# A selective scan of a four-block kernel: its elementwise products taken two units at a time, and one product moved from GpSimd to VectorE

## The chip, the cores and the metric

The kernel runs on one core of a Trainium2 chip. The metric is the device time of one launch in microseconds (us), as a median of runs. The engines are written as in the profile: PE is TensorE (PEld its weight loads), DVE is VectorE, ACT is ScalarE, POOL is GpSimd, and SP is SyncE, whose queue issues the DMAs here.

## What is computed

The kernel runs four blocks one after the other on a 4 x 96 x 64 x 64 image, all in float32. The change lies in the last, a selective scan over four directions of the image (`_L3_conv_ref`):

```python
xs = jnp.stack([x0, x1, x0[..., ::-1], x1[..., ::-1]], axis=1)
x_dbl = jnp.einsum('bkdl,kcd->bkcl', xs, x_proj_weight)
dts, Bs, Cs = jnp.split(x_dbl, [R, R + N], axis=2)
dts = jnp.einsum('bkrl,kdr->bkdl', dts, dt_projs_weight)
A = -jnp.exp(A_logs.astype(jnp.float32)).reshape(K, D, N)
delta = jax.nn.softplus(dts + dt_projs_bias[None, :, :, None])

def step(h, inp):
    u_t, d_t, B_t, C_t = inp
    h = jnp.exp(d_t[..., None] * A) * h + (d_t * u_t)[..., None] * B_t[:, :, None, :]
    y = jnp.einsum('bkdn,bkn->bkd', h, C_t)
    return (h, y)
```

There are 96 channels d, 16 states n, four directions k and, for each of four images, 4096 positions. What follows sums the directions and normalises.

## The kernel before

`selective_scan` cuts the positions into chunks of N = 512. One chunk of one direction is a *step*; there are 4 images x 4 directions x 8 chunks = 128 steps n. In a step the 96 x 16 pairs of channel and state are twelve *units* i of 128 partitions x 512 positions (8 channels x 16 states each). `step` is written out once for each engine and every engine works strictly in the order in which its own `step` lists the work; semaphores tie the engines together. `n1` and `n2` stand for the next step and the one after it, `before` for the previous one.

In words, per step:

- PE: `replicate` (L1669) spreads delta over the 128 partitions of unit i, into one of `DAS` = 3 PSUM tiles `p_da`; since the tile must be free, it waits for scan i - 3. Between the twelve replicates stand: `b_mm` (L1644) and `c_mm` (L1639) of the next step, which replicate B and C; `dt_mm` (L1630), `delta_sum` halves 0 and 1 (L1653 to L1659) and `low_mm` (L1664, L1665), which make delta two steps and one step ahead; four `y_triple` (L1677), each summing the states of three units into `p_y`; and `y_whole` (L1686 to L1690). All of `dt_mm`, `delta_sum`, `low_mm` and `c_mm` write the one PSUM tile `p_bc`, one after the other.
- ACT: `decay` (L1814) takes the exponential in `p_da` for each unit. Between the decays: `delta_and_high` (L1783, L1785), `low` (L1796), `take_y` (L1822 or L1825), the softplus of step n + 2 in pieces (`abs_relu`, `exp_x`, `one_plus`, `kept`, `log_1e`; L1760 to L1776), `c_copy` (L1810) out of `p_bc`, and `b_copy` (L1803).
- DVE: `scan` (L1963) runs the recurrence of a unit, `h` = `p_da` x h + `bu`. Ahead of the scans stand ten `times_b` (L1948), each `bu` = `du_rep` x B for one unit, B being read from PSUM.
- POOL: twelve `times_c` (L1909), each `hc` = `h` x C for one unit; `times_b` (L1902) for units 5 and 11; and `delta_u` (L1891), `du` = delta x u of the next step.
- SP: `restack` (four DMAs that bring delta's two parts into `stacked`, from which PE replicates), `store_du` (one DMA of `du` to DRAM), and twelve `replicate_du` (L1592), which bring `du` back spread over 128 partitions into a ring of `RING` = 8 slots `du_rep`. A slot is written again when its `times_b` has read it.

The delta of step n + 2 goes round the engines in this order: `dt_mm`, `abs_relu` to `log_1e`, `delta_sum` 0 and 1 (half 0 behind `c_copy`), `delta_and_high`, `low_mm`, `low`; only then may the `dt_mm` of the following step write `p_bc`.

## Time and profile before

| | |
|---|---|
| median of 3 runs | 5920.14 us (5917.19 to 5921.82) |
| the profiled execution | 5919.1 us, span of its trace 5917.0 us |
| granted TensorE clock, mean over the span | 0.927 |
| scan, `L1963`, first start to last end | 3253.4 to 5828.9 us |
| busy in the span | PE 4968.7, DVE 4826.2, POOL 3855.9, ACT 2914.8 us |

The scan block is the last 2,600 us but for a short normalisation. A granted clock of 1.00 is 2.4 GHz and 0.50 is 1.2 GHz, the engine's two levels. In a timeline a row is one instruction or several of one kind; matmuls overlap, so from one row of PE the next begins before the first has ended, and the distance of two starts says how long PE was taken.

### The profile page before, as it was taken

The numbers are of one execution on the slowest core, as the hardware profiler recorded it, in microseconds if no ns is written. First come the engines' busy times: TensorE is split into PE (matmuls) and PEld (weight loads), VectorE is DVE, ScalarE is ACT, GpSimd is POOL, SyncE is SP. The second block draws the span as 40 slices with busy tenths as digits, with TensorE's granted clock in tenths as the row PEclk, the third lists the DMA queues.
The fourth block names the chain that finished last, engine by engine and source line by source line (L and its number), as shares of the span: only waits on it lengthen the run. The fifth ranks groups of instructions, "written<-read, shape, count | busy, mean of one in ns | idle before, by whom it ended". The sixth has DMA issues, their size and how long they took to land. (4 is left out here: it accounts for less than half of the span.)

```text
span 5917.0 us, 72829 instructions
## 1 busy us (share of the span) xinstructions
PE 4968.7 (84%) x16018; PEld 2212.0 (37%) x16018; DVE 4826.2 (82%) x4793; ACT 2914.8 (49%) x4462; POOL 3855.9 (65%) x2394
## 2 busy tenths in 40 slices
PE   7999899897699889887068888888888888888887
PEld 1222256463266556555034222222222222222222
DVE  4877633434309999999977999999999999999996
ACT  5777534443201000000023777777777776777776
POOL 0000132322307779777966999999999999999993
PEclk9989899998799889888578999999999999999998
DMA  1000000003864655654041667767676777777773
GB/s 45 0 0 0 7 0 1 0 1 114 229 144 103 135 128 123 136 123 106 0 95 28 182 181 191 187 180 191 187 185 186 187 187 188 186 188 186 186 189 101
DMA packets 340815, 707.92 MB, mean 120 GB/s; under 512 B 46717, under 2 KB 63673, under 8 KB 326745
## 3 DMA queue, kind: packets, MB, share of 16 engines
q1 hardware_dynamic: 340568, 705.15, 47.3%
q8 instruction: 92, 1.51, 0.1%
q14 instruction: 155, 1.26, 0.1%
HBM read 572.97 MB, written 81.67 MB: 111 GB/s over the span
## 5 line engine op out<-in xcount | busy, mean ns | idle before, releaser
L1909 POOL TENSOR_TENSOR l_hc<-l_h,l_c_rep 128x512 f32<-128x512 f32 x1536 | 1927.4, 1273 | 210.5 <-DVE l_h L1963 180.1
L1963 DVE TENSOR_TENSOR_SCAN l_h<-l_p_da,l_h,l_bu 128x512 f32<-128x512 f32 x1120 | 1401.7, 1267 | 6.2 <-ACT l_p_da L1814 4.8
L1814 ACT ACTIVATE l_p_da<-l_p_da,l_a_neg 128x512 f32<-128x512 f32 x1536 | 1008.0, 657 | 724.1 <-PE l_p_da L1669 708.5
L1146 POOL TENSOR_TENSOR l2b_prod<-l2b_v,l2b_attn 128x3136 f32<-128x3136 f32 x114 | 990.1, 8700 | 393.0 <-ACT l2b_attn L1138 369.9
L1669 PE MATMUL l_p_da<-l_stacked,l_pick 96*128 96x512 f32 x1536 | 904.0, 590 | 193.6 <-DVE l_h L1963 184.9
L1948 DVE TENSOR_TENSOR l_bu<-l_du_rep,l_p_b 128x512 f32<-128x512 f32 x1280 | 838.5, 655 | 28.5 <-DMA l_du_rep<-du_scratch 22.6
L1669 PEld LDWEIGHTS l_p_da<-l_stacked,l_pick 96*128 96x128 f32 x1536 | 292.9, 191 | 1165.4 <-DVE l_h L1963 908.1
L1180 DVE TENSOR_REDUCE l2b_osum<-l2b_prod 128x64 f32<-128x3136 f32 x192 | 645.9, 3413 | 2.7
L1677 PE MATMUL l_p_y<-l_hc,l_y_pick 128*32 128x512 f32 x3072 | 560.0, 623 | 72.2 <-POOL l_hc L1909 71.5
L1133 ACT ACTIVATE l2b_logits<-l2b_conv,l2b_this_b 98x512 f32<-98x512 f32 x96 | 66.1, 688 | 912.7 <-PE l2b_conv L1095 912.7
L615 POOL TENSOR_TENSOR l_w_pos_low<-l1a_w_sed,l_w_pos_high 96x1536 fp32r<-96x1536 f32 x1 | 4.1, 4126 | 711.5 <-DVE l_w_fc_high L595 711.5
L1146 DVE TENSOR_TENSOR l2b_prod<-l2b_v,l2b_attn 128x3136 f32<-128x3136 f32 x78 | 386.8, 4959 | 2.5
L1095 PE MATMUL l2b_conv<-l2b_img_high,l2b_w_conv_high 128*98 128x512 f32 x1344 | 349.5, 413 | 33.6 <-DMA l2b_img_low<-qkv_scratch 33.6
L1095 PE MATMUL l2b_conv<-l2b_img_high,l2b_w_conv_low 128*98 128x512 f32 x1344 | 338.8, 403 | 0.0
L1095 PE MATMUL l2b_conv<-l2b_img_low,l2b_w_conv_high 128*98 128x512 f32 x1344 | 337.4, 402 | 0.0
L1902 POOL TENSOR_TENSOR l_pool_bu<-l_du_rep,l_b_sb 128x512 f32<-128x512 f32 x256 | 326.2, 1274 | 0.0
L1963 DVE TENSOR_TENSOR_SCAN l_h<-l_p_da,l_h,l_pool_bu 128x512 f32<-128x512 f32 x224 | 284.5, 1270 | 0.8 <-ACT l_p_da L1814 0.7
L1095 PEld LDWEIGHTS l2b_conv<-l2b_img_high,l2b_w_conv_high 128*98 128x98 f32 x1344 | 226.7, 169 | 140.5 <-issue 31.7
L770 POOL TENSOR_TENSOR l1b_h_h_low<-l1b_h_h,l1b_h_h_high 128x512 fp32r<-128x512 f32 x96 | 125.5, 1319 | 226.8 <-DVE l1b_h_h_high L734 226.8
L1095 PEld LDWEIGHTS l2b_conv<-l2b_img_high,l2b_w_conv_low 128*98 128x98 f32 x1344 | 219.8, 164 | 103.6
L1095 PEld LDWEIGHTS l2b_conv<-l2b_img_low,l2b_w_conv_high 128*98 128x98 f32 x1344 | 219.8, 164 | 102.1
L1297 PE MATMUL l2c_p_x<-l2c_o,l2c_w_proj 96*96 (+1 forms) x64 | 34.6, 626 | 209.7 <-DMA x_back<-x_scratch 209.7
(265 smaller groups left out, 8964.7 us busy)
## 6 DMA issues: line engine op xcount, KB each, us to landing
l_du_rep<-du_scratch SPq DMA_DIRECT2D x1536, 256.0 KB, 3.9
l2b_img_high<-qkv_scratch SPq DMA_DIRECT2D x192, 306.2 KB, 5.5
l2b_img_low<-qkv_scratch SPq DMA_DIRECT2D x192, 306.2 KB, 9.2
l_stacked<-l_parts SPq DMA_DIRECT2D x512, 96.0 KB, 2.7
qkv_scratch<-l2a_strip SPq DMA_DIRECT2D x32, 840.0 KB, 5.1
l2b_v<-qkv_scratch SPq DMA_DIRECT2D x48, 560.0 KB, 16.9
du_scratch<-l_du SPq DMA_DIRECT2D x128, 192.0 KB, 2.2
qkv_scratch<-l2a_v_strip SPq DMA_DIRECT2D x32, 210.0 KB, 4.0
```

What stands on the lines that cost most here:

```text
L770: pool.tensor_tensor(h_hl[1][:, f, :], h[:, f, :], h_hl[0][:, f, :], ALU.subtract).then_inc(s_h_lo, 1)
L1095: mm = pe.matmul(p_conv[n % 2][:], w_conv[w_part][:, g, dx, :], img[x_part][:, hb % 2, row:row + 2 * CP - 1:2, dx:dx + W], start=(at == 0) ...
L1133: act.activation(logits[:, b, CP * ch:CP * (ch + 1), :].rearrange("m p x -> m (p x)"), p_conv[n % 2][:], ACT.Identity, bias=this_b[:]).the ...
L1146: return eng.tensor_tensor(dst.rearrange("q x (dy dx) -> q x dy dx", dx=WIN), window, attn[:, :, r].rearrange("q x (dy dx) -> q x dy dx", ...
L1180: dve.tensor_reduce(osum[:, unit // 2, unit % 2, :], prod[which][:], AX_X, ALU.add).then_inc(s_sum, 1)
L1669: pe.matmul(p_da[i % DAS][:], pick[:, GRP[i] % (Q // DL), :], stacked[:, par, GRP[i] * DL // Q, :], start=True, stop=True).then_inc(s_rep, 1)
L1677: mm = pe.matmul(p_y[par][q * 32:(q + 1) * 32, :], y_pick[:, t, :], hc[:, (G * par + YT * t + q) % HCS, :], start=(t == 0), stop=False)
L1814: act.activation(p_da[i % DAS][:], p_da[i % DAS][:], ACT.Exp, scale=a_neg[:, k * G + GRP[i]:k * G + GRP[i] + 1]).then_inc(s_da, 1)
L1902: pool.tensor_tensor(pool_bu[:, at, :], du_rep[:, ring_at(par, i)], b_sb[:], ALU.mult).then_inc(s_pbu, 1)
L1909: pool.tensor_tensor(hc[:, (G * par + i) % HCS, :], h[:, i, :], c_rep[:, par, :], ALU.mult).then_inc(s_hc, 1)
L1948: dve.tensor_tensor(bu[:, i % BUS, :], du_rep[:, ring_at(par, i)], p_b[par][:], ALU.mult).then_inc(s_bu, 1)
L1963: dve.tensor_tensor_scan(h[:, i, way], p_da[i % DAS][:, way], of, state, ALU.mult, ALU.add).then_inc(s_h, 1)
```

## The change

- `times_b` and `times_c` treat two units (a *duo*, numbered 0 to 5) in one instruction of 128 x 1024 elements; B or C is read twice through an access pattern with a stride of zero (`both`).
- DVE does `times_b` for duos 0, 1, 3 and 4, POOL for duos 2 and 5 (units 4, 5, 10, 11). `pool_bu` is one duo, `bu` two.
- `delta_u` goes from POOL to DVE, behind scan 1. There it reads delta from `p_bc` itself, adds `ln_one` and multiplies by u in one instruction. So `low_mm`, which overwrites `p_bc`, gets a wait for `s_du`, and ACT's `delta_and_high` loses its own.
- DVE's order: `scan` first, then the `times_b` of the duo ahead. POOL's: the last `times_c` of a step stands at the head of the next.
- PE's order: `b_mm` now behind replicate 0, `y_triple` 2 of the step before behind replicate 1, `low_mm` behind replicate 3, `y_triple` 0 behind replicate 7, `y_triple` 1 behind replicate 11 and ahead of `delta_sum` half 1. ACT's `low` stands behind decay 4. Scan and `y_triple` wait for whole duos of `hc`.

```diff
@@ -1424,11 +1424,12 @@
...
-    BUS = 3
...
-    ON_POOL = (5, 11)
-    BU_AHEAD = 4
-    NB = G - len(ON_POOL)
+    DUOS = G // 2
+    ON_POOL = (2, 5)
+    ON_VECTOR = (0, 1, 3, 4)
+    BUS = 2
+    NB, NPB = len(ON_VECTOR), len(ON_POOL)
...
+        def both(a):
+
+            return bass.AP(a.tensor, a.offset, [list(a.ap)[0], [0, 2], [1, N]])
...
-                user, step_of = (i - RING) % G, (i - RING) // G
+                user, step_of = (i - RING) % G // 2, (i - RING) // G
                 if user in ON_POOL:
-                    sp_.wait_ge(s_pbu, len(ON_POOL) * (n + step_of) + ON_POOL.index(user) + 1 + PBU0)
+                    sp_.wait_ge(s_pbu, NPB * (n + step_of) + ON_POOL.index(user) + 1 + PBU0)
                 else:
-                    sp_.wait_ge(s_bu, NB * (n + step_of) + vector_bus(user) + 1 + BU0)
+                    sp_.wait_ge(s_bu, NB * (n + step_of) + ON_VECTOR.index(user) + 1 + BU0)
...
@@ -1661,6 +1666,8 @@
             def low_mm(m):
                 pe.wait_ge(s_hi, m + 1 + HI0)
                 pe.nop(nofuse=True)
+                pe.wait_ge(s_du, m + 1 + DU0)
+                pe.nop(nofuse=True)
                 pe.matmul(p_bc[0:C, :], ident[:], dd[:], start=True, stop=False)
                 pe.matmul(p_bc[0:C, :], minus_r[:], parts[:, 0, :], start=False, stop=True).then_inc(s_lomm, 1)
...
             def y_triple(n, t, par):
-                pe.wait_ge(s_hc, G * n + YT * t + YT + HC0)
+                pe.wait_ge(s_hc, DUOS * n + duos_hold(YT * t + YT) + HC0)
...
                 for i in range(G):
                     replicate(n, i, par)
-                    if before and i == 0:
+                    if n1 and i == 0:
+                        b_mm(n + 1, 1 - par, *n1)
+                    if before and i == 1:
                         y_triple(n - 1, 2, 1 - par)
-                    if n1 and i == 1:
-                        b_mm(n + 1, 1 - par, *n1)
-                    if n1 and i == 2:
+                    if n1 and i == 3:
                         low_mm(n + 1)
                     if before and i == 3:
                         y_triple(n - 1, 3, 1 - par)
@@ -1711,14 +1718,14 @@
                         y_whole(n - 1, *before, 1 - par)
                     if n2 and i == 5:
                         dt_mm(n + 2, *n2, n + 1)
-                    if i == 6:
+                    if i == 7:
                         y_triple(n, 0, par)
                     if n1 and i == 8:
                         c_mm(n + 1, *n1, n2)
-                    if i == 9:
-                        y_triple(n, 1, par)
                     if n2 and i == 10:
                         delta_sum(n + 2, n + 2, 0)
+                    if i == 11:
+                        y_triple(n, 1, par)
                     if n2 and i == 11:
                         delta_sum(n + 2, None, 1)
...
             def delta_and_high(m, par):
                 act.wait_ge(s_d, m + 1)
                 act.nop(nofuse=True)
-                act.wait_ge(s_du, m + DU0)
-                act.nop(nofuse=True)
                 act.activation(dd[:], p_bc[0:C, :], ACT.Identity, bias=ln_one[:])
...
                     decay(n, k, i)
                     if n1 and i == 0:
                         delta_and_high(n + 1, 1 - par)
-                    if n1 and i == 3:
+                    if n1 and i == 4:
                         low(n + 1)
                     if before and i == 5:
                         take_y(n - 1, *before, 1 - par)
...
-            def delta_u(m, b, k, c):
-                pool.wait_ge(s_hi, m + 1 + HI0)
...
-                pool.tensor_tensor(du[:], dd[:], u_of(b, k, c), ALU.mult).then_inc(s_du, 1)
...
+            def times_b(n, duo, par):
+                at, i = ON_POOL.index(duo), 2 * duo
...
+                for j in (i, i + 1):
+                    pool.wait_ge(s_dur[ring_at(par, j)], ring_count(n, par, j))
...
+                user, step_of = 2 * ON_POOL[at - 1], -1 if at == 0 else 0
+                if step_of == 0 or not (isinstance(n, int) and n == 0):
+                    pool.wait_ge(s_h, G * (n + step_of) + user + 2 + H0)
+                pool.tensor_tensor(pool_bu[:], du_rep[:, ring_at(par, i):ring_at(par, i) + 2, :],
+                                   both(b_sb[:]), ALU.mult).then_inc(s_pbu, 1)
...
+            def times_c(n, duo, par):
+                i = 2 * duo
+                if duo == 0:
                     pool.wait_ge(s_ccp, n + 1 + CCP0)
...
+                pool.wait_ge(s_h, G * n + i + 2 + H0)
+                pool.wait_ge(s_ymm, TRIPLES * n + (i + 1 - HCS) // YT + 1 + YMM0)
+                slot = (G * par + i) % HCS
+                pool.tensor_tensor(hc[:, slot:slot + 2, :], h[:, i:i + 2, :], both(c_rep[:, par, :]), ALU.mult).then_inc(s_hc, 1)
...
-                    if i + BU_AHEAD in ON_POOL:
-                        times_b(n, i + BU_AHEAD, par)
-                    if n1 and i == 2:
-                        delta_u(n + 1, *n1)
-                    times_c(n, i, par)
...
+                if before:
+                    times_c(n - 1, DUOS - 1, 1 - par)
+                for duo in range(DUOS - 1):
+                    if duo == 0:
+                        times_b(n, ON_POOL[0], par)
+                    if duo == 2:
+                        times_b(n, ON_POOL[1], par)
+                    times_c(n, duo, par)
...
         @block.vector
...
+            def delta_u(m, b, k, c):
+                dve.wait_ge(s_hi, m + 1 + HI0)
...
+                dve.wait_ge(s_dus, 16 * m + DUS0)
...
+                dve.scalar_tensor_tensor(du[:], p_bc[0:C, :], ln_one[:], u_of(b, k, c), ALU.add, ALU.mult).then_inc(s_du, 1)
...
+            def times_b(n, duo, par):
+                at, i = ON_VECTOR.index(duo), 2 * duo
...
+                for j in (i, i + 1):
+                    dve.wait_ge(s_dur[ring_at(par, j)], ring_count(n, par, j))
+                user, step_of = 2 * ON_VECTOR[(at - BUS) % NB], (at - BUS) // NB
+                if step_of == 0 or not (isinstance(n, int) and n == 0):
+                    dve.wait_ge(s_h, G * (n + step_of) + user + 2 + H0)
+                dve.tensor_tensor(bu[:, at % BUS], du_rep[:, ring_at(par, i):ring_at(par, i) + 2, :],
+                                  both(p_b[par][:]), ALU.mult).then_inc(s_bu, 1)
...
             def step(b, n, k, c, par, n1, n2, before):
...
                 for i in range(G):
-                    if i < G - 1 and i + 1 not in ON_POOL:
-                        times_b(n, i + 1, par)
-                    if i == G - 1 and n1:
+                    scan(n, k, c, i, par)
+                    if n1 and i == 1:
+                        delta_u(n + 1, *n1)
+                    if i % 2 == 0 and i + 2 < G and i // 2 + 1 in ON_VECTOR:
+                        times_b(n, i // 2 + 1, par)
+                    if i == G - 2 and n1:
                         times_b(n + 1, 0, 1 - par)
-                    scan(n, k, c, i, par)
-
+
+            delta_u(0, 0, 0, 0)
             times_b(0, 0, 0)
```

On PE at the end of a step, before: replicate 11, the second half of `delta_sum`, then the next step's replicate 0 (which first waits for `stacked`) and `y_triple` 2.

```order
L1668 REGISTER_ALU
L1669 MATMUL l_p_da<-l_stacked,l_pick 128x512 [waits l3_h]
L1656 MATMUL l_p_bc<-l_kept_e,l_minus 96x512
L1659 MATMUL l_p_bc<-l_one_e,l_ident 96x512 [waits l3_log_of_one_plus_e]
L1668 ISA [waits l3_stacked1]
L1669 MATMUL l_p_da<-l_stacked,l_pick 128x512 [waits l3_h]
L1673 ISA
L1677 MATMUL l_p_y<-l_hc,l_y_pick 32x512 [waits l3_hc]
```

The same place after the change:

```order
L1675 REGISTER_ALU
L1676 MATMUL l_p_da<-l_stacked,l_pick 128x512 [waits l3_h]
L1680 REGISTER_ALU
L1684 MATMUL l_p_y<-l_hc,l_y_pick 32x512 [waits l3_hc]
L1684 MATMUL l_p_y<-l_hc,l_y_pick 32x512 x2
L1661 MATMUL l_p_bc<-l_kept_e,l_minus 96x512
L1664 MATMUL l_p_bc<-l_one_e,l_ident 96x512 [waits l3_log_of_one_plus_e]
L1675 ISA [waits l3_stacked1]
L1676 MATMUL l_p_da<-l_stacked,l_pick 128x512 [waits l3_h]
```

`y_triple` 1 (the L1684 rows), which stood two units earlier, now lies between replicate 11 and `delta_sum` half 1; the next step's replicate 0 stands behind both.

On PE around `low_mm` (the matmuls on `l_dd` and `l_parts`), before:

```order
L1669 MATMUL l_p_da<-l_stacked,l_pick 128x512 [waits l3_h]
L1662 REGISTER_ALU
L1664 MATMUL l_p_bc<-l_dd,l_ident 96x512 [waits l3_delta_and_high]
L1665 MATMUL l_p_bc<-l_parts,l_minus_r 96x512
L1668 REGISTER_ALU
L1669 MATMUL l_p_da<-l_stacked,l_pick 128x512 [waits l3_h]
L1673 REGISTER_ALU
L1677 MATMUL l_p_y<-l_hc,l_y_pick 32x512 [waits l3_hc]
L1677 MATMUL l_p_y<-l_hc,l_y_pick 32x512 x2
L1668 REGISTER_ALU
```

and after:

```order
L1675 REGISTER_ALU
L1676 MATMUL l_p_da<-l_stacked,l_pick 128x512 [waits l3_h]
L1667 REGISTER_ALU
L1671 MATMUL l_p_bc<-l_dd,l_ident 96x512 [waits l3_delta_and_high,l3_du]
L1672 MATMUL l_p_bc<-l_parts,l_minus_r 96x512
L1680 REGISTER_ALU
L1684 MATMUL l_p_y<-l_hc,l_y_pick 32x512 [waits l3_hc]
L1684 MATMUL l_p_y<-l_hc,l_y_pick 32x512 x2
L1675 REGISTER_ALU
L1676 MATMUL l_p_da<-l_stacked,l_pick 128x512 [waits l3_h]
```

`low_mm` has moved behind replicate 3, so that it is followed at once by `y_triple` 3 and then by replicate 4, and it waits for `l3_du` too.

On DVE at the head of a step, where that `du` comes from (scans are printed as SCALAR_TENSOR_TENSOR on `l_h`); after the change, from `delta_u` on:

```order
L1949 ISA [waits l3_du_stored]
L1949 SCALAR_TENSOR_TENSOR l_du<-l_p_bc,l_ln_one,x_back 96x512
L1967 REGISTER_ALU
L1968 REGISTER_ALU [waits l3_da]
L1975 REGISTER_ALU [waits l3_hc]
L1978 SCALAR_TENSOR_TENSOR l_h<-l_p_da,l_h,l_bu 128x512 [waits l3_bu]
L1967 REGISTER_ALU
L1978 SCALAR_TENSOR_TENSOR l_h<-l_p_da,l_h,l_bu 128x512 [waits l3_bu,l3_hc,l3_da]
L1967 REGISTER_ALU
L1968 REGISTER_ALU [waits l3_da]
L1971 ISA [waits l3_hc]
L1978 SCALAR_TENSOR_TENSOR l_h<-l_p_da,l_h,l_pool_bu 128x512 [waits l3_pool_bu]
```

Before, every scan but two had a `times_b` of one unit ahead of it and `delta_u` stood on POOL:

```order
L1947 REGISTER_ALU [waits l3_du_replicated2]
L1948 TENSOR_TENSOR l_bu<-l_du_rep,l_p_b 128x512 [waits l3_h]
L1955 REGISTER_ALU [waits l3_da]
L1960 REGISTER_ALU [waits l3_hc]
L1963 SCALAR_TENSOR_TENSOR l_h<-l_p_da,l_h,l_bu 128x512 [waits l3_bu]
L1947 REGISTER_ALU [waits l3_du_replicated3]
L1948 TENSOR_TENSOR l_bu<-l_du_rep,l_p_b 128x512 [waits l3_h]
L1955 REGISTER_ALU [waits l3_da]
```

## Rows read from the trace of the kernel before

**Rows 1.** Windows, one step: busy time of PE, PEld, DVE, ACT, POOL, then granted clock, DMA.

```profile
4522.64:4542.72 20.08, 17.56 (x57) 5.73 (x55) 20.08 (x23) 14.56 (x25) 18.68 (x16) 1.00 0.69 192
```

**Rows 2.** Timeline of DVE: start us, us, engine, line, operation, tiles.

```profile
4522.64 1.26 DVE L1963 TENSOR_TENSOR_SCAN l_h<-l_p_da,l_h,l_bu 128x512 f32<-128x512 f32 x1
4523.84 0.65 DVE L1948 TENSOR_TENSOR l_bu<-l_du_rep,l_p_b 128x512 f32<-128x512 f32 x1
...
4527.96 2.44 DVE L1963 TENSOR_TENSOR_SCAN l_h<-l_p_da,l_h,l_bu 128x512 f32<-128x512 f32 x2
```

**Rows 3.** Timeline of PE, first half of the step.

```profile
4520.61 1.06 PE L1677 MATMUL l_p_y<-l_hc,l_y_pick 128*32 128x512 f32 x6
4521.60 0.50 PE L1669 MATMUL l_p_da<-l_stacked,l_pick 96*128 96x512 f32 x1
...
4522.40 0.80 PE L1669 MATMUL l_p_da<-l_stacked,l_pick 96*128 96x512 f32 x1
4523.03 1.02 PE L1664 MATMUL l_p_bc<-l_dd,l_ident 96*96 96x512 f32 x2
...
4524.13 0.39 PE L1669 MATMUL l_p_da<-l_stacked,l_pick 96*128 96x512 f32 x1
...
4525.73 0.50 PE L1669 MATMUL l_p_da<-l_stacked,l_pick 96*128 96x512 f32 x1 [0.23 <-DVE l_h L1963]
4526.07 1.87 PE L1690 MATMUL l_p_y<-l_y_sum,l_ident 96*96 96x512 f32 x2
```

**Rows 4.** Timeline of ACT in the same step.

```profile
4525.14 0.58 ACT L1796 ACTIVATE l_parts<-l_p_bc 96x512 fp32r<-96x512 f32 x1
...
4528.21 0.66 ACT L1814 ACTIVATE l_p_da<-l_p_da,l_a_neg 128x512 f32<-128x512 f32 x1 [1.28 <-PE l_p_da L1669]
...
4529.81 0.66 ACT L1814 ACTIVATE l_p_da<-l_p_da,l_a_neg 128x512 f32<-128x512 f32 x1
...
4531.86 0.66 ACT L1814 ACTIVATE l_p_da<-l_p_da,l_a_neg 128x512 f32<-128x512 f32 x1 [0.21 <-PE l_p_da L1669]
...
4535.81 0.58 ACT L1810 ACTIVATE l_c_rep<-l_p_bc 128x512 f32<-128x512 f32 x1
...
4540.79 0.66 ACT L1814 ACTIVATE l_p_da<-l_p_da,l_a_neg 128x512 f32<-128x512 f32 x1 [1.29 <-PE l_p_da L1669]
```

**Rows 5.** Timeline of PE, end of the step.

```profile
4536.64 1.07 PE L1653 MATMUL l_p_bc<-l_relu_x,l_ident 96*96 96x512 f32 x2 [0.37 <-ACT l_c_rep L1810]
```

**Rows 6.** Groups of POOL by shape (count, busy us, mean ns of one).

```profile
L1909 POOL TENSOR_TENSOR l_hc<-l_h,l_c_rep 128x512 f32<-128x512 f32 x1536 | 1927.4, 1273 | 210.5 <-DVE l_h L1963 180.1 <-issue 24.4
L1146 POOL TENSOR_TENSOR l2b_prod<-l2b_v,l2b_attn 128x3136 f32<-128x3136 f32 x114 | 990.1, 8700 | 393.0 <-ACT l2b_attn L1138 369.9 <-DVE l2b_osum L1180 23.2
...
L955 POOL TENSOR_TENSOR l2a_strip<-l2a_qk,l2a_strip 96x1024 fp32r<-96x1024 f32 x32 | 73.8, 2307 | 109.5 <-DVE l2a_strip L915 109.5
```

**Rows 7.** Groups of DVE by shape.

```profile
L747 DVE SCALAR_TENSOR_TENSOR x_front<-l1b_h_p_x,l_cols,l1b_h_x 96x512 f32<-96x512 f32 x32 | 36.1, 1129 | 54.1 <-PE l1b_h_p_x L645 54.1
...
L1343 DVE SCALAR_TENSOR_TENSOR l2c_x<-l2c_p_x,l2c_cols,x_back 96x512 f32<-96x512 f32 x32 | 23.5, 734 | 15.7 <-PE l2c_p_x L1297 15.7
```

**Rows 8.** A window in which the granted clock fell (columns as in rows 1).

```profile
4563.00:4566.00 3.00, 3.00 (x9) 0.98 (x9) 1.95 (x3) 0.68 (x2) 0.00 (x0) 0.50 0.09 23
```

**Rows 9.** Timeline of PE about this window.

```profile
4562.51 0.51 PE L1669 MATMUL l_p_da<-l_stacked,l_pick 96*128 96x512 f32 x1 [1.97 <-DVE l_h L1963]
4562.94 1.93 PE L1677 MATMUL l_p_y<-l_hc,l_y_pick 128*32 128x512 f32 x6
...
4566.29 0.80 PE L1669 MATMUL l_p_da<-l_stacked,l_pick 96*128 96x512 f32 x1
```

**Rows 10.** Timeline of the DMA queue SP (rows merged).

```profile
4527.14 2.45 SPq L1566 DMA_DIRECT2D l_stacked<-l_parts  x4
...
4532.22 12.88 SPq L1592 DMA_DIRECT2D l_du_rep<-du_scratch  x11
```

**Rows 11.** The page: DMA issues, KB each, median us to landing.

```profile
l_du_rep<-du_scratch SPq DMA_DIRECT2D x1536, 256.0 KB, 3.9
```

66 lines of the change are left out of this document (25 added, 41 removed).

## The prediction

> **What bounds the kernel now.** The sum is made against the profiled execution, 5919.1 us, of which the trace spans 5917.0; it lies 1 us under the median, so both are read as one. I read a window of one step first [rows 1]: 20.08 us, the distance of two scans of unit 0. DVE is busy for all of it, POOL for 18.68, PE for 17.56, ACT for 14.56, and the granted clock is 1.00. The 128 steps make 2,570 of the 5,917 us; all else in the kernel is untouched.
>
> DVE's timeline [rows 2] shows how its step adds up. The next instruction starts 1.20 us after a scan's start, and two scans in a row show 2.44 with one full 1.26 in it, so 1.18; I take 1.19. Twelve are 14.28, and the rest of 20.08 over ten `times_b` is 0.58 each. DVE sets the pace.
>
> But PE and ACT have a chain of their own through the one tile `p_bc`, and it is nearly as long. Its two slack places: replicate 4 waits 0.23 for DVE [rows 3], and the decay 7 waits 0.21 on PE [rows 4]. I look at this chain because the change touches it twice.
>
> **What the change takes from DVE.** Ten `times_b` of 0.58 are 5.8. The trace has no 128 x 1024 product on DVE. A 512 product costs 0.58 here, of which I can't tell the fixed part. Two of them, 1.16, are the upper bound; twice as many elements can't cost less than 1.5 times (0.87), which I call an estimate. I take 1.11, near the upper end, since 0.58 for 512 elements leaves little that is fixed. Four are 4.44. `delta_u` on DVE is new: the same operation with the same operands in PSUM and SBUF took 734 ns in one block and 1129 in another [rows 7]. I take 0.74 for its result and 0.62 until DVE's next instruction, as a recorded 0.65 product has 0.58. DVE's sum: 14.28 + 4.44 + 0.62 = 19.34, 0.74 less than 20.08. If DVE still set the pace, 128 x 0.74 = 95 us would be saved.
>
> A rule of the Trainium skill promises more: "VectorE: DVE Perf Modes", section "The TRN2 errata", says that a large tile pays the fixed latency once where many small ones pay it each time, and its formula has 151 cycles of it, 0.157 us. By that, an estimate from the page, eight units in four instructions instead of eight save 0.63 us in a step, where my 4.44 against 8 x 0.58 = 4.64 saves 0.20; DVE's step would be 18.9. The trace speaks against so much: at 0.58 for the whole of a 512 product its fixed part must lie mostly beside the scan.
>
> **POOL.** Fifteen instructions go, eight of 1024 elements come. The nearest row is 2307 ns for 96 x 1024 [rows 6]; two of 1273 would be 2.55. Eight are 18.5 to 20.4 us. `times_b` of duo 5 now waits for scan 5, since `pool_bu` is one duo, and behind it stand `times_c` 2 to 4; POOL is idle there in any case if a step takes more than 20.4.
>
> **The chain through `p_bc`.** Here two things are added.
>
> First, `low_mm` now waits for `delta_u`, which DVE reaches only behind scan 0, `times_b` 1 and scan 1; scan 0 needs decay 0, which needs replicate 0, which stands on PE behind `delta_sum` half 1. Behind `low_mm` on PE are queued `y_triple` 3 and replicate 4, for which decay 4 and scan 4 wait; then `y_whole` and `dt_mm`, for which the whole softplus on ACT waits.
>
> Second, `y_triple` 1 now stands between replicate 11 and `delta_sum` half 1, that is inside the chain; before it stood where PE had time.
>
> The ring, from scan 0 to the next scan 0, in a step whose `y_whole` reads the turned `y_sum`:
>
> - scan 0, `times_b` 1, scan 1: 1.19 + 1.11 + 1.19 = 3.49
> - `delta_u` 0.74, and 0.15 until PE has passed its wait: 0.89 (an estimate: PE starts 4536.64 - 4535.81 - 0.58 = 0.25 behind ACT's `c_copy` [rows 4, 5], with two waits to pass there)
> - `low_mm` until the matmul behind it: 4523.03 to 4524.13, 1.10 [rows 3]
> - `y_triple` 3 until the replicate behind it: 4520.61 to 4521.60, 0.99 [rows 3]
> - replicate 4, `y_whole`, replicate 5 until decay 5: 4525.73 to 4528.21, 2.48 [rows 3, 4]
> - ACT from decay 5 to `c_copy`: 4528.21 to 4535.81, less the wait of 0.21: 7.39 [rows 4]; ACT has no other gap there
> - from `c_copy` over `delta_sum` 0, replicate 11, `delta_sum` 1 and replicate 0 to decay 0: 4535.81 to 4540.79, 4.98 [rows 4, 5]
> - `y_triple` 1, new in there: 0.99
> - decay 0 until the scan: 0.66 and some 0.04
>
> Sum: 3.49 + 0.89 + 1.10 + 0.99 + 2.48 + 7.39 + 4.98 + 0.99 + 0.70 = **23.0 us**, 3.7 above what DVE needs. In the other half of the steps (directions 0 and 2, contiguous `y_sum`) the way over decay 4, `low` (0.58 until the next, rows 4), `dt_mm` and replicate 6 to decay 6 decides: replicate 4 to decay 4 0.53, `low` 0.58, wake 0.75, `dt_mm` 1.10, replicate 0.53, then 4529.81 to 4535.81 less 0.21, 5.79: 9.28 in the place of 2.48 + 7.39, **22.4 us**. The mean is 22.7. (0.53 is replicate to its decay, 0.75 `low`'s duration with its wake: both estimates from 0.50 in rows 3 and 0.58 in rows 4.)
>
> As a check, the same sum for the kernel before: without `y_triple` 1, and with decay 0 to `low_mm` being 2.3 (decay 0 stands 20.08 ahead of 4540.79, `low_mm` at 4523.03) instead of 0.70 + 3.49 + 0.89 = 5.08, plus replicate 3 ahead of `y_triple` 3 (0.3) gives 23.0 - 0.99 - 2.8 + 0.3 = 19.5, and 0.44 of waits on DVE and PE makes the 20.08 seen.
>
> **What TensorE's clock does to it.** In the ring PE stands idle twice for long. Replicate 3 may start when scan 0 has ended, 1.3 us behind its start, and is done at 1.8; `low_mm` comes at 3.49 + 0.89 = 4.4, 2.6 us later. `delta_sum` half 0 comes at 17.1 (the ring's sum up to there and 0.8), replicate 10 is done at about 15.1, behind scan 7: 2.0 us. Now PE's waits in a step are 0.23 and 0.37 [rows 3, 5] and the clock is 1.00 [rows 1]. At a place where PE paused 1.97 us for a scan [rows 9], the granted clock in the 3 us behind it was 0.50, which is 1.2 GHz [rows 8]. There `y_triple`, a replicate and `b_mm` took 4562.94 to 4566.29, 3.35 us; at 2.4 GHz they take 4520.61 to 4522.40, 1.79 [rows 3]. One fall thus costs 1.56 us where PE is on the ring, and behind both pauses it is. Two falls in a step: 22.7 + 3.1 = **25.8 us**. 128 x (25.8 - 20.08) = 733, and 5919 + 733 = **6652 us**.
>
> [...]
>
> **DMA.** `low` comes later, 8 us behind scan 0 instead of 3. From `restack` to the first `replicate_du` are 4532.22 - 4527.14 = 5.1 us [rows 10], under 1 more to the second, 3.9 to land [rows 11]: about 18 us behind scan 0, when `times_b` 0 is due at 18.7 (4.3 ahead of the next scan 0: `times_b` 0, scan 11 and some 2.0 of waits for decays 11 and 0) in the 23.0 us ring and later with the clock. It is just hidden; if it landed 1 to 2 us late, the step would be up to 1 us longer.
>
> **Rivals.**
>
> 1. *The ring at full clock.* Pauses of 2 to 2.6 us need not lower the clock each time. 22.7 us a step: 5919 + 128 x 2.63 = **6256 us**.
> 2. *DVE keeps the pace, faster than before.* This needs PE to find `low_mm`'s wait met early, or a ring 3.4 us shorter than summed. It decides as soon as the ring is under 19.34. Then 5919 - 95 = **5824 us**. For it speaks that DVE is busy for 100% of a step now; against it, that each term of the ring is in fixed order.
> 3. *Only half of it binds*, `y_triple` 1 in the chain but not the wait: 19.5 + 0.99 = 20.5, **about 5970 us**; with both errors of the sum, no change.
> 4. *POOL slows down.* In the attention block the 128 x 3136 product took 8700 ns [rows 6], 2.77 ns for an element, while DVE worked beside it. At that rate a duo costs 2.84 and a step 22.7, no more than the ring: 6256 us or the forecast. The Trainium skill ("GPSIMD Engine Reference", "Specifications") puts such contention down to DVE instructions with two SBUF inputs; by that rule it stays away, since every DVE instruction of this scan reads one operand from PSUM.
> 5. *The clock stays at half.* PE's parts of the ring (1.10 + 0.99 + about 2 + about 4 + 0.99) are 9 us and would double: some 31 us, **7300 us**.
>
> **How the numbers follow.** Ring with falls of the clock (24.0 to 28.5 us a step, one to three falls and the bounds of the duo and of `delta_u`): 0.62. Rival 1: 0.24. Rival 5: 0.06. Rival 2: 0.04. Rival 3 or no change: 0.04. Rival 4 adds nothing of its own below that. The predicted time is the likeliest's, 6652. The range from 6220 (22.4 us a step throughout) to 7000 (28.5) leaves out about 0.15. About 0.2% is what a measurement of this kernel can tell from no change. Faster 0.05, same 0.02, slower 0.93.
>
> **What would show it.** In the profile after: a distance of scans of unit 0 over 22 us; PE waiting some 2.6 us on DVE's `delta_u` in front of `low_mm`; ACT's decay 4 waiting about 4 us on PE; DVE idle in front of scan 4 (about 1.2 us) and scan 0 (about 1.8 us), released by ACT's `p_da`; the granted clock in the scan near 0.88 (two falls of 3 us to half in 25.8) instead of 1.00; POOL idle several us a step. If DVE is busy for nearly the whole step the ring was wrong; if the clock stays near 1.00, rival 1 was right. A duo's product on DVE near 1.2 us recorded and on POOL near 2.3 would confirm the prices.

## The result: 15.5% slower

| | before | after |
|---|---|---|
| median, us | 5920.69 (4 runs, 5917.19 to 5921.82) | 6836.83 (4 runs, 6827.68 to 6844.59) |
| profiled execution, its span | 5919.1, 5917.0 | 6830.65, 6828.8 |
| mean granted clock of the span | 0.927 | 0.838 |
| distance of two scans of unit 0, mean of 127 | 20.13 | 27.32 |

The ratio is 1.1548, with a 95% interval of 1.1528 to 1.1568. The scan alone accounts for it: 128 x (27.32 - 20.13) = 920 us, and the medians differ by 916. The forecast was 6652 in a range from 6220 to 7000, so the direction and the range were right, and the size was 185 us short.

### The profile after

The page, costliest groups (line, engine, operation, out<-in, shapes, count | busy us, mean ns | idle before, releaser). They answer to [rows 6, 7].

```profile
L1911 POOL TENSOR_TENSOR l_hc<-l_h,l_c_rep 128x1024 f32<-128x1024 f32 x768 | 1794.1, 2349 | 583.3 <-DVE l_h L1978 544.0
L1819 ACT ACTIVATE l_p_da<-l_p_da,l_a_neg 128x512 f32<-128x512 f32 x1536 | 999.6, 657 | 1670.6 <-PE l_p_da L1676 1655.7
...
L1978 DVE TENSOR_TENSOR_SCAN l_h<-l_p_da,l_h,l_pool_bu 128x512 f32<-128x512 f32 x448 | 572.8, 1279 | 529.4 <-ACT l_p_da L1819 523.4
...
L1901 POOL TENSOR_TENSOR l_pool_bu<-l_du_rep,l_b_sb 128x1024 f32<-128x1024 f32 x256 | 606.5, 2369 | 561.3 <-DVE l_h L1978 521.4
...
L1960 DVE TENSOR_TENSOR l_bu<-l_du_rep,l_p_b 128x1024 f32<-128x1024 f32 x512 | 612.6, 1196 | 13.7 <-DMA l_du_rep<-du_scratch 13.0
L1671 PE MATMUL l_p_bc<-l_dd,l_ident 96*96 96x512 f32 x256 | 214.2, 933 | 320.5 <-DVE l_du L1949 320.5
```

Read it from the idle times. `low_mm` (L1671) waits 320.5 us on `l_du`; that is 2.5 us in each of the 128 steps, and a wait that the kernel before does not have. ACT's decays wait 1656 us on the replicates, POOL's two groups more than 1,000 on the scans, and the scans of DVE 790 on ACT (523 of them in the group shown, 227 and 39 in two more groups of scans). Everyone waits for the next engine of the ring, and no engine is the bound. Only 13 us of DVE's idle time ahead of its pairs comes from a DMA: the transfers of `du_rep` stayed hidden, as the forecast had them.

A stretch of 1,000 us of the scan; the columns are start:end, length, then busy time (and count) of PE, PEld, DVE, ACT, POOL, the granted clock, the DMA share and GB/s. The kernel before:

```profile
4500.00:5500.00 1000.00, 872.99 (x2735) 287.56 (x2733) 994.37 (x1095) 726.09 (x1210) 926.22 (x747) 0.99 0.71 186
```

The kernel after:

```profile
4500.00:5500.00 1000.00, 791.75 (x1985) 247.42 (x1985) 706.89 (x615) 513.82 (x874) 674.79 (x290) 0.78 0.52 136
```

DVE falls from 99% busy to 71%, and the clock from 0.99 to 0.78. So the change takes its work off the engine that bound the kernel, and that engine then stands idle for more than it saved.

Within one step, the timeline of PE (start us, duration, ..., and in brackets the idle time ahead with its releaser):

```profile
4509.88 0.77 PE L1676 MATMUL l_p_da<-l_stacked,l_pick 96*128 96x512 f32 x2
4513.19 2.00 PE L1671 MATMUL l_p_bc<-l_dd,l_ident 96*96 96x512 f32 x2 [2.54 <-DVE l_du L1949]
...
4515.54 1.93 PE L1684 MATMUL l_p_y<-l_hc,l_y_pick 128*32 128x512 f32 x6
...
4524.13 0.80 PE L1676 MATMUL l_p_da<-l_stacked,l_pick 96*128 96x512 f32 x1
4526.23 0.80 PE L1676 MATMUL l_p_da<-l_stacked,l_pick 96*128 96x512 f32 x1 [1.30 <-DVE l_h L1978]
4528.12 1.99 PE L1658 MATMUL l_p_bc<-l_relu_x,l_ident 96*96 96x512 f32 x2 [1.09 <-ACT l_c_rep L1815]
```

And the same step in slices (columns as above):

```profile
4508.80:4513.00 4.20, 1.85 (x9) 0.52 (x8) 4.19 (x5) 2.72 (x5) 2.68 (x2) 0.90 0.14 16
4513.00:4516.00 3.00, 2.81 (x6) 0.88 (x9) 2.40 (x3) 0.00 (x0) 2.34 (x2) 0.50 0.51 153
4516.00:4520.00 4.00, 4.00 (x11) 1.19 (x6) 0.89 (x1) 1.17 (x2) 1.92 (x1) 0.63 0.00 0
4520.00:4524.00 4.00, 3.33 (x13) 1.14 (x12) 4.00 (x5) 3.84 (x7) 1.23 (x1) 1.00 0.52 148
4524.00:4528.00 4.00, 1.72 (x4) 0.48 (x2) 4.00 (x4) 3.97 (x8) 4.00 (x3) 0.73 0.47 154
4528.00:4532.00 4.00, 3.88 (x5) 1.30 (x5) 2.92 (x3) 0.93 (x2) 4.00 (x2) 0.50 1.02 251
4532.00:4536.00 4.00, 4.00 (x10) 1.02 (x10) 1.28 (x1) 0.66 (x1) 1.65 (x2) 0.50 1.01 243
```

Two falls, one behind each group of pauses: 2.54 us ahead of `low_mm`, then 1.30 and 1.09 us ahead of replicate 10 and `delta_sum` half 0. The clock is at its lower level of 1.2 GHz (0.50) as soon as the work resumes. `y_triple`, six products, takes 1.93 us there and 1.06 at 2.4 GHz. A slice's mean clock gives its time at half: (1 - 0.90) x 2 x 4.2 = 0.84, then 3.0, then (1 - 0.63) x 2 x 4 = 2.96, so the first fall holds for 6.8 us, and the second for 2.16 + 8 = 10.2 and more. What it does downstream, on ACT and then on DVE:

```profile
4518.23 0.66 ACT L1819 ACTIVATE l_p_da<-l_p_da,l_a_neg 128x512 f32<-128x512 f32 x1 [6.57 <-PE l_p_da L1676]
```

```profile
4519.11 1.28 DVE L1978 TENSOR_TENSOR_SCAN l_h<-l_p_da,l_h,l_pool_bu 128x512 f32<-128x512 f32 x1 [3.70 <-ACT l_p_da L1819]
```

### The profile page after: what moved, and what is told of

Same layout as the page of the kernel before. It is cut to its first block and busy times, and to the rows that moved or that the text cites. A ratio compares the mean times of both kernels' runs of the same rounds, so it can differ in the third digit from the quotient of the medians.

```text
span 6828.8 us, 69015 instructions
## 1 busy us (share of the span) xinstructions
PE 5476.9 (80%) x16018; PEld 2329.0 (34%) x16018; DVE 4769.8 (70%) x4153; ACT 2881.8 (42%) x4462; POOL 3861.0 (57%) x1498
## 3 DMA queue, kind: packets, MB, share of 16 engines
q14 instruction: 136, 1.11, 0.1%
## 5 line engine op out<-in xcount | busy, mean ns | idle before, releaser
L1911 POOL TENSOR_TENSOR l_hc<-l_h,l_c_rep 128x1024 f32<-128x1024 f32 x768 | 1794.1, 2349 | 583.3 <-DVE l_h L1978 544.0
L1978 DVE TENSOR_TENSOR_SCAN l_h<-l_p_da,l_h,l_bu 128x512 f32<-128x512 f32 x896 | 1107.8, 1267 | 322.4 <-ACT l_p_da L1819 227.2
L1676 PE MATMUL l_p_da<-l_stacked,l_pick 96*128 96x512 f32 x1536 | 1071.6, 725 | 230.0 <-DVE l_h L1978 227.8
L1978 DVE TENSOR_TENSOR_SCAN l_h<-l_p_da,l_h,l_pool_bu 128x512 f32<-128x512 f32 x448 | 572.8, 1279 | 529.4 <-ACT l_p_da L1819 523.4
L1901 POOL TENSOR_TENSOR l_pool_bu<-l_du_rep,l_b_sb 128x1024 f32<-128x1024 f32 x256 | 606.5, 2369 | 561.3 <-DVE l_h L1978 521.4
L1684 PE MATMUL l_p_y<-l_hc,l_y_pick 128*32 128x512 f32 x3072 | 708.1, 776 | 4.4 <-POOL l_hc L1911 4.4
L1676 PEld LDWEIGHTS l_p_da<-l_stacked,l_pick 96*128 96x128 f32 x1536 | 330.8, 216 | 1034.4 <-DVE l_h L1978 552.4
L1960 DVE TENSOR_TENSOR l_bu<-l_du_rep,l_p_b 128x1024 f32<-128x1024 f32 x512 | 612.6, 1196 | 13.7 <-DMA l_du_rep<-du_scratch 13.0
L1671 PE MATMUL l_p_bc<-l_dd,l_ident 96*96 96x512 f32 x256 | 214.2, 933 | 320.5 <-DVE l_du L1949 320.5
L1658 PE MATMUL l_p_bc<-l_relu_x,l_ident 96*96 96x512 f32 x256 | 248.5, 1073 | 148.2 <-ACT l_c_rep L1815 141.5
```

The source lines that it names most:

```text
L1658: pe.matmul(p_bc[0:C, :], ident[:], relu_x[:], start=True, stop=False)
L1671: pe.matmul(p_bc[0:C, :], ident[:], dd[:], start=True, stop=False)
L1676: pe.matmul(p_da[i % DAS][:], pick[:, GRP[i] % (Q // DL), :], stacked[:, par, GRP[i] * DL // Q, :], start=True, stop=True).then_inc(s_rep, 1)
L1684: mm = pe.matmul(p_y[par][q * 32:(q + 1) * 32, :], y_pick[:, t, :], hc[:, (G * par + YT * t + q) % HCS, :], start=(t == 0), stop=False)
L1901: pool.tensor_tensor(pool_bu[:], du_rep[:, ring_at(par, i):ring_at(par, i) + 2, :], both(b_sb[:]), ALU.mult).then_inc(s_pbu, 1)
L1911: pool.tensor_tensor(hc[:, slot:slot + 2, :], h[:, i:i + 2, :], both(c_rep[:, par, :]), ALU.mult).then_inc(s_hc, 1)
```

## The experiments

All of them are read by the same four numbers: the time, the distance of the scans of unit 0, its mean over those steps that hold no time at half clock (which gives the order of the work at full clock, with nothing of the clock in it), and the falls for each step in the trace's record of the granted clock. The falls are counted in the 112 inner steps, without the first and the last eight; the means are over all 127. Where the ratio says "single run", the time is that of one execution; the kernel before was measured on the same chips at 5920.9 to 5924.8 us. The edits are given in short: what only follows from them, such as a helper that moves along, is left out.

| kernel | us | ratio (95%) | mean step | steps at full clock: number, mean | falls a step | clock 4500 to 5500 |
|---|---|---|---|---|---|---|
| before | 5920.7 | 1 | 20.13 | 105, 20.05 | 0.14 | 0.99 |
| after | 6836.8 | 1.155 (1.153, 1.157) | 27.32 | none | 1.76 | 0.78 |
| no_du_wait | 6317.8 | single run | 23.25 | 9, 20.47 | 1.05 | 0.86 |
| y1_early | 6824.0 | single run | 27.25 | none | 2.00 | 0.79 |
| filler6 | 6502.5 | single run | 24.69 | 31, 23.25 | 0.74 | 0.92 |
| both_undone | 6085.0 | 1.026 (1.024, 1.028) | 21.48 | 30, 20.32 | 0.72 | 0.89 |
| before_du_dve | 6431.7 | single run | 24.15 | 3, 21.47 | 1.38 | 0.87 |
| before_y1_late | 6285.9 | single run | 23.01 | none | 1.02 | 0.87 |
| filler10 | 6565.4 | single run | 25.18 | 28, 23.45 | 0.78 | 0.92 |
| filler_spare | 6295.5 | single run | 23.06 | 126, 23.07 | 0.00 | 1.00 |
| pairs_on_dve | 5990.0 | 1.011 (1.010, 1.013) | 20.59 | 32, 19.83 | 0.71 | 0.92 |
| pairs_y0_late | 5965.1 | 1.009 (1.007, 1.011) | 20.42 | 51, 19.81 | 0.58 | 0.93 |
| pairs_fill | 5895.5 | 0.996 (0.995, 0.997) | 19.93 | 121, 19.83 | 0.02 | 1.00 |
| before_fill | 5933.3 | 1.002 (1.000, 1.003) | 20.23 | 107, 20.01 | 0.12 | 0.99 |

The theory is the forecast's: a ring of fixed order through `low_mm`, longer than DVE's work, and in it two pauses of PE that drop the clock. The rivals: only one of the two additions matters, or the clock falls for another reason than the pauses.

### Taking the wait out of the changed kernel (no_du_wait)

```
 low_mm:
-    pe.wait_ge(s_du, m + 1 + DU0)
 delta_and_high (ACT):
+    act.wait_ge(s_du, m + DU0)
 delta_u (DVE):
-    dve.scalar_tensor_tensor(du[:], p_bc[0:C, :], ln_one[:], u_of(b, k, c), ALU.add, ALU.mult)
+    dve.tensor_tensor(du[:], dd[:], u_of(b, k, c), ALU.mult)
```

> The changed kernel with delta_u on VectorE still, but reading dd in SBUF as before, so that low_mm does not wait for it (ACT's delta_and_high waits for the delta_u of the step before, as it did). Theory (ring through p_bc): scan 0, times_b 1, scan 1 and delta_u leave the ring; it falls from 23.0/22.4 to about 20.6 us at full clock, and PE's pause in front of low_mm goes, so the clock falls about half as often: 22.3 us a step with falls, about 6200 us (5990 if the clock stayed at 2.4 GHz throughout). Rival A (the two-unit instructions themselves hold the step, by GpSimd's and the hc semaphores' coarser grain): stays within 2% of 6837. Rival B (the two SBUF inputs of the new delta_u slow GpSimd beside it): GpSimd's two-unit product above 2.5 us.

Measured: 6317.8 us, 519 less than after. It lies 118 us above the 6200 that the theory had, and rival B came in part: the POOL pair that starts beside `delta_u` took 2.64 us, as shown below, the mean of all pairs of `times_c` 2404 ns. Its nine steps at full clock take 20.47 us, against 23.07 in the kernel that keeps the wait (filler_spare, below). So the wait is worth some 2.6 us a step at full clock, as far as nine steps can tell, and the rest of its 4.07 us is clock. It is the larger half of the loss.

### Putting y_triple 1 back in the changed kernel (y1_early)

```
                 if i == 8: c_mm(...)
+                if i == 9:
+                    y_triple(n, 1, par)
                 if i == 10: delta_sum(n + 2, n + 2, 0)
-                if i == 11:
-                    y_triple(n, 1, par)
```

> The changed kernel with y_triple 1 back behind replicate 9, ahead of delta_sum half 0; all else as changed. Theory (ring): y_triple's 1.0 us leaves the stretch from c_copy to decay 0, but behind replicate 9 PE now waits for GpSimd's duo 2, which gives part of it back: 22.6 us at full clock, about 24.9 us with fewer falls of the clock, about 6540 us. Rival (only the wait for delta_u matters): 6837 within 1%.

Measured: 6824.0 us, 0.2% less than after, where the theory had about 6540. This is a miss, and the traces show its reason. PE has a new pause of 2.54 us at the early place. PE:

```profile
4514.26 0.80 PE L1676 MATMUL l_p_da<-l_stacked,l_pick 96*128 96x512 f32 x1
4517.60 1.93 PE L1684 MATMUL l_p_y<-l_hc,l_y_pick 128*32 128x512 f32 x6 [2.54 <-POOL l_hc L1911]
```

And POOL, on which it waits:

```profile
4512.87 2.37 POOL L1901 TENSOR_TENSOR l_pool_bu<-l_du_rep,l_b_sb 128x1024 f32<-128x1024 f32 x1 [3.44 <-DVE l_h L1978]
4515.20 6.96 POOL L1911 TENSOR_TENSOR l_hc<-l_h,l_c_rep 128x1024 f32<-128x1024 f32 x3
```

`times_b` of duo 5 waits 3.44 us for scan 5 and then takes 2.37, and `times_c` of duo 2, which `y_triple` 1 reads, stands behind it. The forecast had named this order on POOL ("behind it stand `times_c` 2 to 4; POOL is idle there in any case") but followed it only as POOL's own time, not to the PE instruction that waits for its result. With POOL's order as it is, `y_triple` 1 therefore can't come early in the changed kernel: its late place is no cost that can be given back by itself.

### Both, and POOL's order (both_undone)

```
   no_du_wait, y1_early, and
 step (POOL):
-    if duo == 2:
+    if duo == 3:
         times_b(n, ON_POOL[1], par)
```

> The changed kernel's two-unit instructions and delta_u on VectorE (reading dd in SBUF, no wait in low_mm), y_triple 1 back behind replicate 9, and GpSimd's times_b of duo 5 one place later, behind times_c 2, so that PE's y_triple 1 does not wait for it. Theory: the ring is about 19.7 us, VectorE's work 19.4, few falls of the clock: 19.8 to 20.2 us a step, 5880 to 5940 us, about level with the kernel before (ratio 0.995 to 1.003). Rival A (the two-unit form itself is slow): over 6400 us.

Measured: 6085.0 us, ratio 1.026 (1.024 to 1.028), where 5880 to 5940 was expected: a miss of 150 us. Two things make it. The larger is the clock, which still falls 0.72 times a step: 128 x (21.48 - 20.32) = 148 us. Of the 81 falls counted 60 stand at scans 4 and 5, where PE waits 0.85 us for `l_hc` ahead of `y_triple` 0; the kernel before waits 0.55 us ahead of the same instruction. PE's waits for `l_hc` are 50.5 us in the stretch 4500 to 5500, 1.1 us a step, against 27.8 us and 0.6 a step before. That these waits are the cause of the falls is not shown by itself, since PE's waits in all are not longer than before. And `delta_u`, which in this kernel reads two operands in SBUF, costs more than its row promised. Timeline of DVE in both_undone:

```profile
4502.79 1.84 DVE L1949 TENSOR_TENSOR l_du<-l_dd,l_xt 96x512 f32<-96x512 f32 x1
```

Of POOL at the same time:

```profile
4501.72 2.37 POOL L1901 TENSOR_TENSOR l_pool_bu<-l_du_rep,l_b_sb 128x1024 f32<-128x1024 f32 x1
4504.05 2.81 POOL L1911 TENSOR_TENSOR l_hc<-l_h,l_c_rep 128x1024 f32<-128x1024 f32 x1
```

In no_du_wait, where POOL happens to be idle when `delta_u` starts, DVE and POOL:

```profile
4518.61 0.67 DVE L1949 TENSOR_TENSOR l_du<-l_dd,x_back 96x512 f32<-96x512 f32 x1
```

```profile
4518.86 2.64 POOL L1911 TENSOR_TENSOR l_hc<-l_h,l_c_rep 128x1024 f32<-128x1024 f32 x1 [2.23 <-DVE l_h L1978]
```

Whichever starts first keeps its time, and the other is stretched, here and in the means over all steps. Behind a running POOL product `delta_u` takes 1.84 us and ends 0.54 behind it (4504.63 against 4504.09); its mean over the 128 steps is 1553 ns against 666 in no_du_wait (124 of the 128 start behind a running POOL product, against 5). The POOL product that starts during `delta_u` takes 2.81 or 2.64 instead of 2.37. That is 0.9 us a step on DVE in both_undone: the forecast's 19.34 us of DVE work and 0.9 make 20.2, next to the 20.32 of its steps at full clock. The Trainium skill ("GPSIMD Engine Reference", "Specifications") puts contention of the two engines down to DVE instructions with two SBUF inputs, or in a 2-port perf mode, which no run here tests. The traces agree on the first. With an operand in PSUM neither engine is stretched: in the changed kernel `delta_u` takes 722 ns and the POOL product that starts beside it 2.34 to 2.37 us, and in before_du_dve (below), where `delta_u` starts behind a running POOL product in 127 of 128 steps, it takes 722 ns again and that product 1.27 us, as always.

### Each part alone, in the kernel before (before_du_dve, before_y1_late)

before_du_dve:

```
 low_mm:
+    pe.wait_ge(s_du, m + 1 + DU0)
 POOL step:
-    if n1 and i == 2:
-        delta_u(n + 1, *n1)
 DVE step:
     scan(n, k, c, i, par)
+    if n1 and i == 1:
+        delta_u(n + 1, *n1)       # scalar_tensor_tensor out of p_bc
 delta_and_high (ACT):
-    act.wait_ge(s_du, m + DU0)
```

> The kernel before with one part of the change alone: the product delta times u runs on VectorE behind scan 1, out of PSUM, and low_mm waits for it (ScalarE's wait for it is gone). Theory (the ring of the scan closes through delta_u, and PE's pause there drops the clock): the ring replicate, decay, scan, delta_u, low_mm is 21.6 us a step at full clock, and with a fall or so per step 23 to 24.5, so 6250 to 6450 us. Rival (the wait in low_mm is harmless as long as VectorE is not in pairs): VectorE's own work grows by 0.6 us a step, 128 x 0.6 = 80 us, so about 6000 us, and the granted clock in the scan stays near 0.99.

Measured: 6431.7 us. The theory held, to 20 us of its upper end; the rival had 6000. Without a single pair, the wait in `low_mm` costs 511 us: 1.4 us a step at full clock (21.47 against 20.05, from three steps only), and 1.38 falls a step.

before_y1_late:

```
-                if i == 9:
-                    y_triple(n, 1, par)
                 if n2 and i == 10:
                     delta_sum(n + 2, n + 2, 0)
+                if i == 11:
+                    y_triple(n, 1, par)
```

> The kernel before with y_triple 1 moved from behind replicate 9 to behind replicate 11, between the halves of delta_sum; nothing else. Theory (the place puts 1 us of y_triple into PE's own queue behind the last replicates, and makes a pause of PE ahead of it): steps of 20.5 us at full clock against 20.1, and with a fall or so 22.9; 5970 us without falls, 6280 us with. Rival (the place costs nothing because the scan has slack there, as the kernel with the order put back within the change showed nothing): within 20 us of before, clock near 0.99 in the scan.

Measured: 6285.9 us, where the theory had 6280 with falls of the clock. Four lines, no operation added or removed, and 365 us. The timeline of PE:

```profile
4512.65 0.50 PE L1669 MATMUL l_p_da<-l_stacked,l_pick 96*128 96x512 f32 x1 [1.27 <-DVE l_h L1963]
...
4514.47 1.91 PE L1654 MATMUL l_p_bc<-l_e_x,l_ident 96*96 96x512 f32 x2
```

Its slice right behind (columns as above):

```profile
4515.00:4518.00 3.00, 3.00 (x9) 0.53 (x7) 3.00 (x4) 0.66 (x1) 2.63 (x3) 0.54 1.07 251
```

Where `y_triple` 1 stood, PE now has a pause of 1.27 us ahead of replicate 10, in addition to 0.42 and 0.37 us about it. The clock falls in nearly every step there (108 falls of the 114 counted stand at scans 7 and 8), and only then come the `delta_sum` halves and the moved `y_triple`, all of them on the ring. So a place in PE's order that looks free holds the clock up. No step ran at full clock, so how much of the 365 us is ring and how much clock stays open. In the changed kernel y1_early could not take this addition back; between no_du_wait and both_undone, which differ in it and in POOL's order, lie 233 us.

### Filling PE's pauses (filler6, filler10, filler_spare)

If the pauses drop the clock, then work without use in them must bring it back and leave the ring. filler6, ahead of replicates 3 and 10, behind their waits:

```
 replicate:
     pe.wait_ge(s_h, G * n + i + 1 - DAS + H0)
+    if i in (3, 10):
+        for _ in range(6):
+            pe.matmul(p_da[i % DAS][:], ...)      # the replicate itself, repeated
```

> The changed kernel with six extra copies of the replicate matmul of units 3 and 10 (same operands, same p_da tile, ahead of the real one), 1.3 us each time, in the pauses of PE in front of low_mm and of delta_sum half 0. Theory (pauses drop the clock, and that costs the 4.5 us a step above the 22.7 us ring): the granted clock in the scan rises from 0.78 to over 0.93 and the step falls to about 23.5 us, about 6360 us, although PE has more to do. Rival (the ring is simply longer than summed and the clock is incidental): no gain, or the filler's time on top, 6837 us or more.

Measured: 6502.5 us, 334 less than after, by adding work; falls 0.74 in place of 1.76. The 31 steps without a fall take 23.25 us. The time expected was 6360, so this is a miss by 140 us: the clock rose to 0.92 and not over 0.93, and the falls left were open.

filler10 is the same with ten repeats for unit 3 and eight for unit 10.

> The changed kernel with the pauses of PE filled further: 10 extra copies of the replicate product ahead of unit 3 and 8 ahead of unit 10 (about 2.1 and 1.7 us of PE work at 2.4 GHz), results overwritten. Theory (the clock falls come from the pauses; the rest is the ring at full clock): falls per step from 0.74 to 0.2 or fewer, steps of 23.2 to 23.7 us, 6320 to 6400 us. Rival (the falls left are set by something else than these two pauses): granted clock in the scan stays near 0.92 and the time at or above 6500 us.

Measured: 6565.4 us, a miss; the rival's numbers came (clock 0.92, falls 0.78, "at or above 6500"). But all 87 falls counted stand at scans 7 and 8, and the timeline shows a pause of 1.46 us there, ahead of the repeats: they stand behind replicate 10's wait, and so can't fill it. The ones of unit 3 worked. So the third version writes into the half of `p_y` that is free at the time, and stands ahead of the waits:

```
+def fill(n, half, at, par, count):
+    pe.wait_ge(s_y, n + at + Y0)
+    for _ in range(count):
+        pe.matmul(p_y[half][:], pick[:, 0, 0:C], stacked[:, par, 0, :], start=True, stop=True)
                 if n1 and i == 3:
+                    fill(n, par, -1, par, 10)
                     low_mm(n + 1)
+                if i == 9:
+                    fill(n, 1 - par, 0, par, 6)
                 if n2 and i == 10:
+                    fill(n, 1 - par, 0, par, 5)
                     delta_sum(n + 2, n + 2, 0)
```

> The changed kernel with its three pauses of PE filled by products of 96 x 512 into the half of p_y that nobody uses at the time: 10 ahead of low_mm, 6 behind replicate 9 (ahead of the wait for scan 7, which the earlier filler stood behind), 5 ahead of delta_sum's first half. Their results are overwritten. Theory (all falls of the clock come from these pauses; without them the step is the ring, 23.2 to 23.5 us): falls per step from 0.78 to under 0.2, granted clock in the scan 0.98 or more, 128 x (23.35 - 20.13) + 5920 = about 6330 us (6310 to 6380). Rival (the falls that the earlier filler left come from something else): clock in the scan still about 0.92 and 6500 us or more.

Measured: 6295.5 us, no fall in the scan, clock 1.00, 23.06 us a step. The theory had 6310 to 6380; the clock did what it said, and the time is 15 us under its lower end. This divides the loss in two: 128 x (23.06 - 20.13) = 375 us are the ring at full clock, and 128 x (27.32 - 23.06) = 545 us are the clock.

### The pairs alone (pairs_on_dve, pairs_y0_late, pairs_fill, before_fill)

Is anything of the change worth having? pairs_on_dve takes the kernel before, and only DVE's products with B become pairs:

```
-ON_POOL = (5, 11);  BUS = 3
+ON_POOL = (10, 11); BUS = 2; DUOS = 5
 DVE step:
-    if i < G - 1 and i + 1 not in ON_POOL:
-        times_b(n, i + 1, par)
     scan(n, k, c, i, par)
+    if i % 2 == 0 and i // 2 + 1 < DUOS:
+        times_b(n, i // 2 + 1, par)               # 128 x 1024
+    if i == G - 2 and n1:
+        times_b(n + 1, 0, 1 - par)
```

> From the kernel before, only the good half of the change: VectorE multiplies by B two units per instruction for units 0 to 9 (5 instructions of 128 x 1024), each behind a scan; GpSimd keeps its single-unit products with C, takes B for units 10 and 11, and keeps delta times u; the order of PE and ScalarE stays. Theory (the change loses by its ring, VectorE in pairs saves only where nothing else closes): VectorE's work per step falls from 12 x 1.19 + 10 x 0.58 to 12 x 1.19 + 5 x 1.11 us, 0.25 us less, and the step is 19.8 us at full clock, 20.1 to 20.2 with few falls: 5885 to 5930 us, ratio 0.994 to 1.002. Rival (longer instructions make PE and GpSimd wait longer for the first scan of a pair): slower than before by 1% or more, over 5980 us.

Measured: 5990.0 us, ratio 1.011 (1.010 to 1.013): slower, where the theory had 0.994 to 1.002. But its 32 steps at full clock take 19.83 us, 0.22 less than before's. (The expectations further down have 19.95 and 20.06 for the two; their 33 steps include one with a time at half clock.) With a pair between scans 4 and 5, replicate 8 waits:

```profile
4517.01 0.50 PE L1670 MATMUL l_p_da<-l_stacked,l_pick 96*128 96x512 f32 x1 [1.57 <-DVE l_h L1970]
```

and 74 of the 80 falls stand right behind it. Two ways to treat this pause. pairs_y0_late moves `y_triple` 0 into it:

```
-                if i == 6:
+                if i == 7:
                     y_triple(n, 0, par)
```

> The same kernel with pairs on VectorE, without filler; y_triple 0 of PE moves from behind replicate 6 to behind replicate 7, so that the 1.54 us pause ahead of replicate 8 becomes two of about 0.8 us. Theory (short pauses as the kernel before has them, 0.7 to 1.0 us, start few falls): falls per step from 0.71 to 0.2 or fewer, 5885 to 5925 us. Rival (the clock goes by how idle PE is about that place and not by the length of one pause): falls stay near 0.7 a step, 5970 to 5990 us.

Measured: 5965.1 us. The pause became two of 0.69 and 0.81 us, and the falls went only from 0.71 to 0.58 a step. That is the rival's answer: halving the pause did not save the clock. pairs_fill puts six products there instead (`fill(n, 1 - par, 0, par, 6)` behind replicate 7):

> The kernel with only VectorE's products with B in pairs (5990 us), and six products of 96 x 512 into the unused half of p_y in PE's pause of 1.54 us ahead of replicate 8, behind which 74 of its 80 falls stand. Theory (what this kernel lost is the half clock, the pairs themselves gain): 0 to 0.2 falls a step, steps as its own 33 steps without a fall, 19.95 us, against before's mean of 20.13: 128 x (19.95 - 20.13) = -23, so 5885 to 5915 us, ratio 0.994 to 0.999. Rival (the pairs lose by their own waits): stays within 15 us of 5990.

```profile
4506.48 1.56 PE L1676 MATMUL l_p_y<-l_stacked,l_pick 96*96 96x512 f32 x6
4508.20 0.50 PE L1670 MATMUL l_p_da<-l_stacked,l_pick 96*128 96x512 f32 x1 [0.16 <-DVE l_h L1977]
```

```profile
4500.00:5500.00 1000.00, 918.29 (x3065) 333.97 (x3063) 991.71 (x854) 738.95 (x1221) 933.82 (x754) 1.00 0.73 188
```

Measured: 5895.5 us, ratio 0.996 (0.995 to 0.997), inside the expected 5885 to 5915, and faster than both kernels. Clock 1.00, steps of 19.83 us, DVE busy for 99% again. The control puts the same six products into the kernel before, without pairs:

> Control for the last pair: the kernel before with the same six products of 96 x 512 behind replicate 7, and no pairs. Theory (the 0.4% of the kernel with pairs and filler is the pairs': 19.83 us for its steps without a fall against 20.06 for before's): filler alone can save at most before's own falls, 128 x (20.13 - 20.06) = 9 us, and its 1.28 us of PE work stands where before's PE pauses 0.39 us only, so it may cost up to 0.9 us a step: 5910 to 6035 us. Rival (the filler is the gain): 5895 us or less.

Measured: 5933.3 us, ratio 1.002 (1.000 to 1.003). So the filler alone gains nothing; the 0.2 us a step come with the pairs, once the clock is kept. DVE's sum says the same: 12 x 1.19 + 5 x 1.11 = 19.83, where ten single products make 20.08. The kernels with pairs differ from before in DVE's order and in the units that POOL takes, too (10 and 11 for 5 and 11); no run has these without the pairs.

## Why the prediction was right, and what it mis-sized

**The ring.** It is right in kind, and its terms can be read in filler_spare, where no clock disturbs them. One step of direction 0 or 2, DVE:

```profile
4457.78 1.28 DVE L1987 TENSOR_TENSOR_SCAN l_h<-l_p_da,l_h,l_bu 128x512 f32<-128x512 f32 x1 [2.04 <-ACT l_p_da L1828]
...
4461.28 0.72 DVE L1958 SCALAR_TENSOR_TENSOR l_du<-l_p_bc,l_ln_one,x_back 96x512 f32<-96x512 f32 x1
...
4480.89 1.28 DVE L1987 TENSOR_TENSOR_SCAN l_h<-l_p_da,l_h,l_bu 128x512 f32<-128x512 f32 x1 [2.04 <-ACT l_p_da L1828]
```

PE:

```profile
4462.15 1.07 PE L1671 MATMUL l_p_bc<-l_dd,l_ident 96*96 96x512 f32 x2 [0.27 <-DVE l_du L1958]
...
4463.38 1.06 PE L1689 MATMUL l_p_y<-l_hc,l_y_pick 128*32 128x512 f32 x6
4464.37 0.50 PE L1676 MATMUL l_p_da<-l_stacked,l_pick 96*128 96x512 f32 x1
```

ACT:

```profile
4468.16 0.66 ACT L1828 ACTIVATE l_p_da<-l_p_da,l_a_neg 128x512 f32<-128x512 f32 x1 [1.00 <-PE l_p_da L1676]
...
4473.85 0.58 ACT L1824 ACTIVATE l_c_rep<-l_p_bc 128x512 f32<-128x512 f32 x1
...
4479.98 0.66 ACT L1828 ACTIVATE l_p_da<-l_p_da,l_a_neg 128x512 f32<-128x512 f32 x1 [2.44 <-PE l_p_da L1676]
```

| term | forecast | measured |
|---|---|---|
| scan 0, pair 1, scan 1 | 3.49 | 3.50 |
| `delta_u` to `low_mm` | 0.89 | 0.87 |
| `low_mm` to `y_triple` 3 | 1.10 | 1.23 |
| `y_triple` 3 to replicate 4 | 0.99 | 0.99 |
| replicate 4 to decay 6, over `low` and `dt_mm` | 3.49 | 3.79 |
| decay 6 to `c_copy` | 5.79 | 5.69 |
| `c_copy` to decay 0, with `y_triple` 1 | 5.97 | 6.13 |
| decay 0 to scan 0 | 0.70 | 0.91 |
| sum | 22.4 | 23.11 |

No term is off by more than 0.3 us, and the sum by 0.7; the largest is the stretch that was put together from estimates instead of being read. The forecast's check of the same sum against the kernel before was short in the same direction: 19.5 and 0.44 are 19.9, and not the 20.08 seen. The median step of directions 0 and 2 is 22.92. In directions 1 and 3 the median step is 23.28, against a forecast of 23.0. So the mean was 22.7 in the forecast and is 23.06, 46 us for the whole kernel.

**Prices.** A pair on DVE records 1196 ns, and its next instruction starts 1.11 to 1.12 us behind it (4458.98 to 4460.09 is 1.11), as taken. The Trainium skill's fixed term ("VectorE: DVE Perf Modes", "The TRN2 errata"), by which a pair would save 0.16 us over two single products (an estimate from the page: its 0.157 us once instead of twice), is not seen as such: 1.11 against 2 x 0.58 is 0.05. In the kernels with pairs alone the step shrank by 0.2 us for five pairs, which is 0.04 each. `delta_u` took 0.72 (0.74 taken). POOL's pairs took 2349 and 2369 ns, just above the 2307 of the 96-partition row, and not the 2840 of rival 4.

**The pauses** came at the two places, 2.54 us (2.6 forecast) ahead of `low_mm`; the second was forecast as one of 2.0 us ahead of `delta_sum`, and is 1.3 ahead of replicate 10 and 1.1 ahead of `delta_sum`. The signs on ACT and DVE (decay 4 waits, scans 4 and 0 wait on ACT) are all there, lengthened by the clock: 6.57 us ahead of decay 4 where 4 was forecast, 3.70 ahead of scan 4 where 1.2 was. In filler_spare, at full clock, the same two waits are 4.28 and 1.41 us.

**The step that was mis-sized is the clock.** "Two falls in a step: 22.7 + 3.1 = 25.8" is measured as 1.76 falls and 27.32 - 23.06 = 4.26 us, that is 2.4 us a fall instead of 1.56. The number of falls was nearly right. The length was not: the forecast took one window of 3 us [rows 8] and counted only what PE did in it, and the slices of after show stretches of 6.8 and of 10.2 us at 0.50. The one fall it read was a short one: 17 of the 22 falls in the scan of the kernel before end within 4 us, and 187 of the 223 in after last over 6. So it had 6 us at half clock in a step, and 42% of 27.32 is 11.4. Its sign for it was a clock of 0.88 in the scan, and 0.78 is what stands there. How the 127 steps of after sort by their time at half clock:

| us at half clock | under 5 | 5 to 8.5 | 8.5 to 12 | 12 to 15.5 | over 15.5 |
|---|---|---|---|---|---|
| steps | 11 | 21 | 23 | 57 | 15 |
| mean length, us | 24.3 | 26.0 | 27.5 | 27.9 | 29.0 |

The steps of the second group are 3.0 us longer than 23.06, those of the fourth, with about twice the time at half, only 1.8 us longer again. That part of PE's work there is off the ring would explain it; no run shows this by itself.

**The rivals.** Rival 1, the ring at full clock, was forecast at 6256 and is a kernel of its own now: filler_spare, 6295.5. Rival 2 failed, since DVE is 71% busy. Rival 3 (only `y_triple` 1 binds): each of the two additions costs alone, as the two kernels made from before show (511 and 365 us). Its sum was good, 20.5 us a step with `y_triple` 1 in the chain and no wait, which no_du_wait shows as 20.47 at full clock; its time of 5970 was not, since the clock fell there too (6317.8). Rival 4 failed by POOL's 2349 ns. Rival 5, a clock that stays at half, was too dark: 42% of the scan is at half.

**The sum of it.** 375 us ring and 545 us clock, 920 in all; the forecast was 335 and 397.

## What to carry to other kernels

Before making the busiest engine faster, sum the ring that its instructions close with the other engines; work that moves onto it from another engine (here `delta_u`) ties that ring tighter, even where both engines' totals shrink. Count PE's pauses before and after, since a new pause of 1.3 us ahead of PE work on the critical ring cost more here than most instructions do; products without use, put ahead of the wait and into a free bank, gave 541 us back. And where a change gains in some steps and loses in the mean, sort the steps by the clock first: the pairs looked like a loss of 1.1% and were a gain of 0.4% behind one pause.

## What the runs showed of the chip that was not expected

- **Work without use made a kernel faster**: 21 products a step, some 5.3 us of PE time, turned 6836.8 into 6295.5 us.
- **A pause's length alone does not tell whether the clock falls.** Pauses of 1.27 us in before_y1_late are followed by a fall in nearly every step, 1.54 us in pairs_on_dve in two of three, two pauses of 0.69 and 0.81 us in pairs_y0_late in over half, and one of 0.81 ahead of replicate 10 in pairs_fill (in all 112 steps counted) in next to none. What PE did between and ahead of them must count too; these runs do not settle how.
- **A fall lasts longer than its cause**: in after, a pause of 2.54 us is followed by 6.8 us at 0.50.
- **Two SBUF inputs on DVE beside POOL**: one 96 x 512 product went from a mean of 666 to 1553 ns when a POOL product was already running, and a POOL product that started during it from 2.37 to 2.64 and 2.81 us. The same work with one operand in PSUM took 722 ns, behind a running POOL product too (before_du_dve), and left POOL alone.
